# A hand-ordered opening of an attention and feed-forward kernel gets another order on all engines, and plain fp32 products for tile 0

## The reference, cut to what matters

```python
# attention: 8 batches ("tiles") of 128 tokens, 32 query heads in 8 groups (HK), 4 heads per group (REP), 512 cached keys
q = einsum('bsd,ed->bse', x, Wq);  k = einsum(..., Wk);  v = einsum(..., Wv)
q = rope(rmsnorm(q, q_norm_w), pos);  k = rope(rmsnorm(k, k_norm_w), pos)      # pos = cache_seqlens + token
kc = k_cache[block_table];  vc = v_cache[block_table]                          # pages fetched by index
scores = where(valid, q @ [kc, k] * SCALE, -1e30);  probs = softmax(scores);  o = probs @ [vc, v]
attn = o @ Wo
x = x + (prune(silu(attn @ w_gate)) * (attn @ w_up)) @ w_down                  # prune: smallest half of |.| set to 0
x = x + (x @ adapter[ids]) @ int4_weights + bias
```

## Time and profile before

| what | value |
|---|---|
| median of 3 runs | 1374.59 us (1374.22 to 1374.66) |
| span of the profiled execution | 1372.6 us |
| its own time | not listed apart from the runs; the median is 2.0 us above the span |
| TensorE busy | 1356.7 us, 99% of the span |
| VectorE busy | 1204.1 us, 88% |
| ScalarE busy | 871.6 us, 64% |
| GpSimd busy | 785.0 us, 57% |

### The profile page before, as it was taken

How to read it: one execution, slowest core, us unless ns; L and a number is a source line. 1 busy time by engine, 2 the same in 40 slices (tenths; PEclk the granted TensorE clock), 3 DMA queues, 4 the chain that set the end, 5 groups by cost and what they waited for, 6 DMA issues and landing times.

```text
span 1372.6 us, 23448 instructions
## 1 busy us (share of the span) xinstructions
PE 1356.7 (99%) x8015; PEld 1182.3 (86%) x8015; DVE 1204.1 (88%) x2624; ACT 871.6 (64%) x2224; POOL 785.0 (57%) x813
## 2 busy tenths in 40 slices
PE   8899999999999999999999999999999999999998
PEld 6788888888888888888888888888888888888888
DVE  8999898989898989898989898989899987987783
ACT  7777676767676767676767676767777662222221
POOL 7876766676667666766676667666766510111111
PEclk9999999999999999999999999999999999999999
DMA  6111221111112111211111112112121321111212
GB/s 215 48 53 41 59 55 47 43 59 55 47 43 59 54 47 43 58 55 47 43 59 53 49 42 59 55 47 70 49 72 32 110 96 45 47 47 49 76 40 77
DMA packets 34034, 80.46 MB, mean 59 GB/s; under 512 B 10258, under 2 KB 11538, under 8 KB 32498
## 3 DMA queue, kind: packets, MB, share of 16 engines
q1 hardware_dynamic: 17522, 45.29, 10.5%
q0 software_dynamic: 16384, 33.59, 8.4%
HBM read 76.74 MB, written 2.10 MB: 57 GB/s over the span
## 4 chain that ended last, share of the span: by engine, by line
PE 91%; DVE 5%; ACT 2%; issue 1%; POOL 1%; DMA 0%; DVEq 0%; ACTq 0%
PE proj_ps L111 10%; PE proj_ps L113 10%; PE proj_ps L112 10%; PE turn_ps L770 10%; PE score_ps L113 5%; PE score_ps L112 5%; PE score_ps L111 5%; PE value_ps L111 5%; PE value_ps L112 5%; PE value_ps L113 5%; PE gu_ps L111 3%; PE gu_ps L113 3%; PE gu_ps L112 3%; PE out_ps L1035 2%; PE turn_ps L732 2%; PE turn_ps L739 2%
## 5 line engine op out<-in xcount | busy, mean ns | idle before, releaser
L1286 ACT ACTIVATE probs<-probs,shift,rstd 128x640 f32<-128x640 f32 x256 | 234.4, 917 | 123.3 <-DVE shift L1730 122.2
L561 POOL DMA_INDIRECT kg<-kc,idx x256 | 260.1, 1016 | 83.9 <-issue 78.0
L571 POOL DMA_INDIRECT vg<-vc,idx x256 | 260.0, 1016 | 70.7 <-issue 70.7
L1766 DVE TENSOR_TENSOR pt_lo<-turn_ps,pt_hi 128x512 fp32r<-128x512 f32 x320 | 217.4, 685 | 45.2 <-ACT pt_hi L1292 44.8
L1292 ACT ACTIVATE pt_hi<-turn_ps 128x512 fp32r<-128x512 f32 x320 | 187.5, 593 | 90.6 <-PE turn_ps L770 89.3
L1741 DVE CUSTOM_DVE_ANT_0 probs<-score_ps,mask 128x640 f32<-128x640 f32 x256 | 206.8, 822 | 11.9 <-PE score_ps L113 10.1
L579 POOL TENSOR_TENSOR v_lo<-vg,v_hi 128x512 fp32r<-128x512 f32 x64 | 89.1, 1392 | 207.7 <-ACT v_hi L1257 207.7
L770 PE MATMUL turn_ps<-cst,probs 128*128 128x128 f32 x1280 | 191.5, 272 | 0.7 <-DVE qt_lo L1718 0.7
L111 PE MATMUL proj_ps<-w_hi,xt_parts 128*128 128x512 f32 x496 | 188.9, 381 | 0.0
L770 PEld LDWEIGHTS turn_ps<-cst,probs 128*128 128x128 f32 x1280 | 157.2, 141 | 26.9 <-DVE probs L1759 1.0
L113 PE MATMUL proj_ps<-w_hi,xt_parts 128*128 128x512 f32 x496 | 168.1, 339 | 0.0
(11 more groups left out here) (255 smaller groups left out, 3283.4 us busy)
## 6 DMA issues: line engine op xcount, KB each, us to landing
w_raw<-wqkv SPq DMA_DIRECT2D x28, 384.0 KB, 3.2
wo_raw<-wo SPq DMA_DIRECT2D x32, 256.0 KB, 3.0
wa_sb<-wa SPq DMA_DIRECT2D x7, 1024.0 KB, 4.9
kg<-kc,idx POOLq DMA_INDIRECT x256, 2.6
vg<-vc,idx POOLq DMA_INDIRECT x256
wg_raw<-wg SPq DMA_DIRECT2D x2, 1376.0 KB, 6.1
wu_raw<-wu SPq DMA_DIRECT2D x1, 2752.0 KB, 9.6
wd_raw<-wd SPq DMA_DIRECT2D x1, 2560.0 KB, 12.8
```

Of the source, the lines that this page charges most:

```text
L561: pool.indirect_dma_start(kg[:, b % 2, c, :], None, kc, bass.IndirectOffsetOnAxis(ap=idx[:, s // B % 2, b * NC + c:b * NC + c + 1], axis=0))\
L571: pool.indirect_dma_start(vg[:, b % 2, c, :], None, vc, bass.IndirectOffsetOnAxis(ap=idx[:, s // B % 2, b * NC + c:b * NC + c + 1], axis=0))\
L1286: act.activation(row, row, ACT.Exp, bias=shift[:, h:h + 1], scale=rstd[:, b % 2, h:h + 1], accum_out=sums[:, h:h + 1])\
L1766: dve.tensor_tensor(pt_lo[:, at, :], turn_ps[1 - j % 2][:, :], pt_hi[:, at, :].bitcast(F32), ALU.subtract).then_inc(p_lo_done[j], 1)
```

## The change

Only the opening is changed, up to and including step 0, apart from tile 0's x split and a few wait counts.

1. DMA issues. `pages_i`, then the frequencies and lane constants (`cst[:, C_INV:C_KEY]`), then `lens_i`, then the identity matrix are issued by ScalarE, before its first table load, instead of by SyncE. SyncE starts with x tile 0. The q weights of group 0 come in four pieces, one per k, instead of two.
2. Tile 0's projections. TensorE multiplies `x_raw` and `w_raw` directly in fp32, one product per k, instead of three products of rounded parts: 4 instead of 12 for q and 4 instead of 12 for k and v. The split of x tile 0 (ScalarE and VectorE) moves to step 3, where group 1 first needs it. Filler products: 3 instead of 6.
3. VectorE's setup has 7 links ahead of the sines instead of 10: no cast of the lengths, two constants for two pi instead of three, and the mask threshold (`hide_from`) behind them.
4. One head of `normalise` in step 0 and one in step 1 are done by ScalarE (`BY_ACT`).
5. The orders of `steps_ahead()` and `first_step()` differ on TensorE, ScalarE, VectorE and GpSimd.

```diff
-LAST_PIECE = len(W_PIECES) - 1
+W0_PIECES = [(slice(k, k + 1), slice(0, GQ)) for k in range(NK)] + [(slice(0, NK), slice(GQ, GW))]
+BY_ACT = (1, 2)
-SINES_READY = 10
-FILLED = 6
+SINES_READY = 7
+FILLED = 3
 # SyncE
-                    sp.dma_start(cst[:, :], consts[:, 0:C_KEY]).then_inc(const_in, 16)
-                    sp.dma_start(lens_i[:, :], lens).then_inc(const_in, 16)
-                    sp.dma_start(pages_i[:, :], pages).then_inc(pages_in, 16)
 # GpSimd, steps_ahead
                         gather_k(0, 0, 0)
                         gather_k(1, 1, 0)
                         norms(0, 0)
                         gather_v(0, 0)
+                        table(0, 1, 0)
                         norms(1, 1)
-                        gather_k(2, 2, 0)
-                        gather_v(1, 1, ahead)
+                        gather_v(1, 1, range(0, NC // 2))
+                        gather_k(2, 2, 0)
                         split_v(0, 0)
+                        table(0, 1, 1)
+                        table(1, 1, 0)
                         norms(2, 2)
-                        gather_v(1, 1, behind)
-                        table(0, 1, 0)
-                        table(0, 1, 1)
 # TensorE
+                    def first_q():
+                        pe.wait_ge(x_in[0], 16)
+                        for k in range(NK):
+                            pe.wait_ge(w0_in[k], 16)
+                            last = pe.matmul(proj_ps[:, :], x_raw[:, 0, k, :], w_raw[:, k, 0:GQ], start=k == 0,
+                                             stop=k == NK - 1)
+                        last.then_inc(q_chunks, Q_CALLS)
 # TensorE, steps_ahead
-                        pe.wait_ge(const_in, 2 * 16)
-                        first_projections()
+                        first_q()
+                        first_kv()
+                        pe.wait_ge(ident_in, 16)
+                        turn_cached_k(0, 0)
+                        project_q(1, 1, 0, (0, 1))
                         project_q(1, 1, 0, (2,))
-                        turn_cached_k(0, 0)
                         project_q(1, 1, 0, (3,))
...
 # ScalarE
+                    def normalise(s, b, heads):
+                        wait(act, recip_done, s + 1)
+                        for h in heads:
+                            row = probs[:, b % 2, h, :]
+                            act.activation(row, row, ACT.Copy, scale=recips[:, h:h + 1]).then_inc(probs_act_done, 1)
...
+                    act.dma_start(pages_i[:, :], pages).then_inc(pages_in, 16)
+                    act.dma_start(cst[:, C_INV:C_KEY], consts[:, C_INV:C_KEY]).then_inc(const_in, 16)
+                    act.dma_start(lens_i[:, :], lens).then_inc(lens_in, 16)
+                    act.dma_start(ident, consts[:, C_ID:C_ID + P]).then_inc(ident_in, 16)
                     act.wait_ge(setup_pool, 2)
```

More of the change, by code:

```diff
@@ L137, in adaln_attn_ffn @@
         x_in = [semaphore(f"x_in{n}") for n in range(3)]
-        w0_in = [semaphore(f"w0_in{n}") for n in range(3)]
+        w0_in = [semaphore(f"w0_in{n}") for n in range(len(W0_PIECES))]
         w_in = semaphore("w_in")
@@ L185, in adaln_attn_ffn @@
         probs_done = semaphore("probs_done")
+        probs_act_done = semaphore("probs_act_done")
         p_turned = [semaphore(f"p_turned{j}") for j in range(NJ)]
-        p_hi_done = [semaphore(f"p_hi_done{j}") for j in range(NJ)]
+        p_hi_done = semaphore("p_hi_done")
         p_lo_done = [semaphore(f"p_lo_done{j}") for j in range(NJ)]
@@ L662, in first_step @@
                         split_v(1, 1)
+                        table(1, 1, 1)
                         norms(3, 3)
-                        table(1, 1, 0)
-                        table(1, 1, 1)
                         table(0, 2, 0)
                     pool.wait_ge(setup_pool, SETUP_POOL)
-                    ahead, behind = range(0, NC // 2), range(NC // 2, NC)
-                    gather_k(0, 0, 0)
-                    gather_k(1, 1, 0)
-                    norms(0, 0)
-                    gather_v(0, 0)
-                    norms(1, 1)
-                    gather_k(2, 2, 0)
-                    gather_v(1, 1, ahead)
-                    split_v(0, 0)
-                    norms(2, 2)
-                    gather_v(1, 1, behind)
-                    table(0, 1, 0)
-                    table(0, 1, 1)
+                    steps_ahead()
                     first_step()
@@ L697, in project_q @@
                     def project_q(s, b, g, ks):
-                        if b == 0 and ks[0] in (0, 2):
-                            wait(pe, w_lo_done[ks[0] // 2], g + 1)
+                        if b == 0 and g > 0 and ks[0] in (0, 2):
+                            wait(pe, w_lo_done[ks[0] // 2], g)
+                        if s == 1:
+                            wait(pe, w0_lo_done, ks[-1] + 1)
                         if ks[0] == 0:
@@ L716, in project_kv @@
                             if b == 0:
-                                wait(pe, w_lo_done[2], g + 1)
+                                wait(pe, w_lo_done[2], g)
+                            if s == 1:
+                                wait(pe, w0_lo_done, NK + 1)
                             if s < FIRST:
@@ L763, in turn_probs @@
                             wait(pe, probs_done, s + 1)
+                            if s < len(BY_ACT):
+                                wait(pe, probs_act_done, BY_ACT[s])
                             wait(pe, q_lo_done, at_most(s + 2))
@@ new lines, in first_q, with first_kv @@
+                    def first_q():
[5 more added lines that the diff above has]
+                        last.then_inc(q_chunks, Q_CALLS)
+                    def first_kv():
+                        kv = value_ps[:, 0:2 * D]
+                        pe.wait_ge(w0_in[NK], 16)
+                        for k in range(NK):
+                            last = pe.matmul(kv, x_raw[:, 0, k, :], w_raw[:, k, GQ:GW], start=k == 0,
+                                             stop=k == NK - 1)
@@ L1221, in split_w @@
                         ks, cols = W_PIECES[n]
-                        if g == 0:
-                            act.wait_ge(w0_in[n], 16)
-                        else:
-                            wait(act, w_in, g * (NK * 16))
+                        wait(act, w_in, g * (NK * 16))
                         if n < 2:
@@ L1759, in normalise @@
                             last = dve.tensor_scalar(row, row, recips[:, h:h + 1], None, ALU.mult)
-                        if h == REP - 1:
+                        if h == REP - 1 or s < len(BY_ACT) and h == REP - 1 - BY_ACT[s] + (BY_ACT[s - 1] if s else 0):
                             last.then_inc(probs_done, 1)
                     def split_probs(s, b, j):
-                        wait(dve, p_hi_done[j], s + 1)
+                        wait(dve, p_hi_done, NJ * s + j + 1)
                         at = (b + j) % 2
```

217 lines of the change are left out of this document (117 added, 100 removed).

## The result

The changed kernel takes **1377.48 us** (1376.62 to 1377.86, 11 runs) where the kernel before, beside it on the same chip, takes 1374.22 (1373.74 to 1374.66, 11 runs): a ratio of 1.0022, 95% interval 1.0014 to 1.003. It is slower by 3.3 us. The forecast was 1372.3 with a range up to 1375.9, so it was wrong in sign and outside its range. The span of the profiled execution is 1376.1 us, 3.5 more than before, and its own time 1377.86.

A forecast was written before the change was run, and what follows sets the result against it. TensorE bounds the kernel from 63 us on, VectorE from 23.1 to 63, DMA landings matter before. +0.55 + 0.45 - 1.1 - 2.9 + 0.8 - 0.1 = -2.3 us from 1374.6 gave 1372.3 us, range 1369.9 to 1375.9.

The forecast's parts named there:

- the forecast's wait of 4.2 us: TensorE after tile 0's projections: idle from 11.3 to 15.5 us until the gathered keys land, covering 1.0 us extra fp32.
- Keys at 15.5: Gathered keys ready for TensorE's transpose at 15.5 us instead of 16.74; bounds 14.4 and 16.7.
- By the same 2.4 us the index starts at 1.2 + 2.3 = about 3.4: GpSimd's index instruction: old lag from issue to start kept, so start about 3.4 instead of 4.06 us.
- my bounds of 4.7 to 5.7: GpSimd's first gather: between 1.0 us earlier (4.7) and no gain (5.7), taken as 5.0.
- Rival 4: Gathers served only when the x stream lets them: keys stay at 16.7, scores at 24.9, total 1373.5; chance 0.09.
- Rival 2: TensorE's clock falls in the wait for keys and soon returns, holding back 1.55 us: 1373.9; chance 0.20.
- Rival 3: Clock stays low for most of the 8.2 us up to the scores, costing 4.9: 1377.2; chance 0.11.
- Nine products in front of the scores, 2.1: TensorE, keys to scores: nine more q products of tile 1 add 2.1 us, scores start at 23.7.
- Scores to first `pt_lo`, -0.1: VectorE: 0.45 us of new waits between score heads, less 0.55 for a `normalise` head given to ScalarE.
- the 1.55 goes too: VectorE before step 1's `values` product: 1.55 us lost by two `shift`s beside GpSimd's table product disappears.
- -0.55 -2.9 +0.8 -0.1: First `pt_lo` to `values`: second head given away, less VectorE lost time (2.3 for 5.2), TensorE's own queue, small waits.
- Terms that cost nothing: Plain fp32 projections, 1.0 us extra, covered by the wait for keys; x tile 0's split in step 3, under TensorE-bound work.

The follow-up runs named there:

- e3: Changed kernel with five more filler products between tile 0's k and v projection and the transpose of the gathered keys; 1378.5 us, ratio 1.0031.
- f5: Changed kernel with GpSimd's two chains broken up as in f1, nothing else; 1376.81 us.
- f2: Changed kernel with GpSimd's chains broken up as in f1 and the five fillers of e3; 1375.62 us.
- e4: Changed kernel with the edits of e1 and e2 together; 1373.68 us, ratio 1.0002.
- f1: e4 with GpSimd's chains broken up by value gathers moved between split of v and tables; 1374.32 us, ratio 1.0001.
- e2: Changed kernel with pages, lane constants and lengths as SyncE's first three issues, identity behind tile 0's q weights; 1377.31 us, ratio 1.0018.
- e6: Changed kernel with GpSimd's tables (0,1,1) and (1,1,0) behind the second half of step 1's value gathers; 1380.12 us.
- e9: e10 without its second broken chain; 1526.03 us on a chip where the kernel before took 1511 to 1536.
- e10: Same kernel as f1 (e4, both GpSimd chains broken up), on a slow chip; 1520.3 us beside 1524.33, ratio 0.998.
- e12: Same kernel as f2, on a chip where the kernel before took 1511 to 1536 us; 1522.24 us.
- f6: e4 unchanged, run again twelve times; 1374.35 us, four runs from 1375.51 to 1382.56.
- e1: Changed kernel with the transpose of tile 0's gathered keys put back behind nine of tile 1's q products; 1378.51 us, ratio 1.0034.
- e8: Kernel before with GpSimd's tables (0,1,0) and (0,1,1) moved right behind split_v(0); 1375.88 us, ratio 1.0011.
- f3: e1 with the GpSimd edit of f1, constants still on ScalarE's queue; 1374.87 us, ratio 1.0006.
- f4: f1 with split_v(0) one gather later on GpSimd; 1377.16 us, ratio 1.0021.
- e7: Changed kernel with SyncE waiting for pages and lane constants before it issues x and weights; single run, 1380.78 us.
- e11: Same kernel as f3, on a chip where the kernel before took 1511 to 1536 us; 1524.06 us.

## Why the prediction was wrong, point by point

**In one sum.** The `values` product of step 1 was forecast 2.3 us earlier and came 3.5 later, a miss of 5.8. By the marks 1.4 of it lie ahead of the keys, 2.5 between keys and scores, 2.1 between scores and first `pt_lo`, and -0.1 behind that. The largest part is the clock: the sum prices the 8.2 us of products behind the forecast's wait of 4.2 us at full speed and has no term for that wait.

**Keys at 15.5: wrong, 16.87.** The step that failed is "By the same 2.4 us the index starts at 1.2 + 2.3 = about 3.4". The landing time of pages in the old order, where they were issued ahead of x, was carried over to a queue that shares the DMA engines with x and w. It was 3.5 us for the pages and 4.1 for the constants, which the index needs as well. (With 2.4 in place of 2.3 the same line gives 3.6.) The index start was 1.9 us off the forecast and the first gather, with 6.57, outside my bounds of 4.7 to 5.7. The gathers themselves went faster than before (four in 5.6 us instead of 6.34, forecast 5.8), which gave some of it back. Rival 4 had the keys stay at 16.7, but not by its cause: from the end of the fourth gather (12.15) to the transpose it took 4.7 us, as before.

**Rival 2, TensorE's clock: right in mechanism, wrong in chance and price.** The wait that I forecast at 4.2 us was 5.22, and the clock fell. Rows that show no fallen clock were counted as evidence against it, although no wait of that length was in them. I gave "falls" 0.31 in all; behind a wait longer than any in the trace, with the slow start in the earlier trace rows in view, it was the likelier case. Its price, 1.55 us, came from 3.1 us of slow time; it was 5.7 us, and the scores moved by 2.4 to 2.7 (2.5 by the sum of the next point, 2.7 in e3, 2.4 between f5 and f2). Rival 3 put the point of decision at scores after 26 and came to 1377.2. It is the case that happened, but only in part by its own mechanism: the clock gives 1.2 to 1.8, not 4.9.

**Nine products in front of the scores, 2.1: right.** Keys to scores took 10.66 us, which is 6.4 less 0.27 of waiting, 2.1 and 2.5 for the clock.

**Scores to first `pt_lo`, -0.1: wrong, +2.0** (14.82 instead of 12.84). The wait of 0.42 between the maxima and the one of 0.46 behind them, with what the `shift`s add there, make about 1.0 where 0.45 stood. The head given to ScalarE was there (-0.5). The term that is missing is the collision: three heads of `normalise` 2.52 instead of 1.53 (+1.0) and the `shift` 0.85 instead of 0.33 (+0.5). That sum is read from one profile of each; no run here takes the collision out of the changed kernel, so its price there is an estimate.

**"The table products run on GpSimd from about 36.4 to 38.4, beside VectorE instructions that read PSUM, so the 1.55 goes too": this sentence is a failed step as well.** Between those instructions stand `shift`s, whose sources are in SBUF, and a `shift` that had taken 1.82 was in my own. I also looked at the tables alone and not at what stands in front of them: the split of v, right behind which the change puts them, 3.6 us of GpSimd in one piece and beside `normalise`.

**First `pt_lo` to the `values` product: right in sum.** Forecast -0.55 -2.9 +0.8 -0.1 = -2.75, measured 22.5 us instead of 25.4. That gain is real and is what lets e4 and f1 tie with the kernel before, although their first `pt_lo` is 2.3 to 2.8 us later than its.

**Terms that cost nothing** did so: plain fp32 takes 3.60 and 1.99 us ahead of a wait (3.4 and 1.7 forecast), 5.5 together, about 1.3 more than twelve rounded products of 0.23 and twelve of 0.12 where 1.0 was forecast (and 9.4 + 1.7 is 11.1, not the 11.3 that the prediction goes on with; it was 11.65); from 63 us on TensorE is as busy as before, with the split of x tile 0 in step 3.

## What to carry to other kernels

When a reorder leaves TensorE with one wait longer than any in the trace, price the products behind it at half speed first, and take the full speed as the rival. A shorter wait is no safe one: 1.98 us in e2 was enough. Instructions of GpSimd on SBUF should not be lined up without a gap: look at what VectorE does beside the whole chain, down to its smallest instruction with SBUF sources. Here a small DMA landed by what else was in flight more than by when it was issued: one that others wait for belongs ahead of the large ones on every queue.

## What the hardware showed that I had not expected

A VectorE instruction can be held for one GpSimd instruction or for a whole chain. In eleven profiles GpSimd stood idle for 0.34 to 0.70 us ahead of the split of v (the changed kernel, e4 to e6, e9, e10, e12, f1, f2, f5, f6); in each of them the three heads of `normalise` took 2.51 or 2.52 us and the last head got in behind one instruction, whatever followed. In e1, e2, e3 and e8 the split followed a gather without idle time, as that last head came up, with three more instructions behind it, and they took 5.33 or 5.34. In f3 and f4, also without idle time but with a gather behind the small split, it was 3.05 and 3.17, one instruction's wait again. In e7 and e11 the split came when the heads were done, and they took 1.69. Why the idle time or the gather behind lets the head in, I did not test. A `shift` of one column took up to 3.18 us, 20 times its 0.15. And a second fall of the clock came after waits of 3.4 us in e2 and e3 and 3.2 in e8, and not after 3.4 in e1; 1.98 us was enough in e2 and 1.72 was not in e4. What decides it is open too.
